# The first 13 units of the attention maxima, moved from the attention program to the end of the projection program

## What is computed

```python
h = _layernorm(x) * (1 + ca) + sa
q = concat([q_c, rope(q_e)]); k = concat([k_c, rope(k_e)])   # b, 16 heads, 2048, 16
scores = einsum('bhqd,bhkd->bhqk', q, k) * scale
scores = where(causal, scores, -inf)
att = softmax(scores)                                        # needs the row maxima
y = einsum('bhqk,bhkd->bhqd', att, v) @ Wc
```

## Time and profile before

| | us |
|---|---|
| median of 3 runs | 2794.07 (2793.2 to 2794.93) |
| profiled execution, its own time | 2799.72 |
| its span in the trace | 2798.0 |
| mean granted PE clock in it | 0.933 of full |

### The profile page before, as it was taken

The page is one execution under the profiler, slowest core; times in us unless marked ns, Lnnn a source line. Parts: engine busy times, 40 slices in busy tenths (PEclk is TensorE's granted clock), DMA queues, the critical chain, the costliest instruction groups (busy, mean ns, idle before and its releaser), DMA issues. The chain is left out here.

```text
span 2798.0 us, 46776 instructions
## 1 busy us (share of the span) xinstructions
PE 2536.4 (91%) x16092; PEld 1312.3 (47%) x16093; DVE 1906.6 (68%) x3194; ACT 1671.1 (60%) x2989; POOL 745.2 (27%) x692
## 2 busy tenths in 40 slices
PE   6985899999999999999999999999676579879898
PEld 4553233333333333333333333332265479779788
DVE  5985888878878878878888888781066556445433
ACT  2655037777777777777777777778532245435444
POOL 2544300111011011011011011011046747636533
PEclk8998579999999999999999999999887689989999
DMA  5798901541550451452353244000286666546434
GB/s 168 215 250 221 148 16 36 103 73 56 104 100 20 90 101 29 81 101 38 72 101 48 62 77 62 17 17 14 79 237 188 177 149 127 96 82 114 82 63 63
DMA packets 214886, 271.22 MB, mean 97 GB/s; under 512 B 27280, under 2 KB 176304, under 8 KB 212272
## 3 DMA queue, kind: packets, MB, share of 16 engines
q1 hardware_dynamic: 175408, 221.01, 35.8%
q0 software_dynamic: 32160, 41.57, 8.7%
q10 hardware_dynamic: 7136, 6.32, 0.7%
HBM read 136.30 MB, written 131.74 MB: 96 GB/s over the span
## 5 line engine op out<-in xcount | busy, mean ns | idle before, releaser
L1073 DVE TENSOR_REDUCE mxc<-ps 128x2 f32<-128x1024 f32 (+4 forms) x1168 | 1297.8, 1148 | 294.9 <-PE ps L981 182.6
L1054 ACT ACTIVATE probs<-ps 128x512 f32<-128x512 f32 (+1 forms) x2240 | 1184.3, 588 | 401.7 <-PE ps L1011 371.9
L1011 PE MATMUL ps<-qs,ks 99*128 99x512 bf16 (+3 forms) x2560 | 736.5, 350 | 6.5 <-ACT probs L1054 4.5
L981 PE MATMUL ps<-ks,qs 96*128 96x512 bf16 (+3 forms) x2560 | 696.7, 362 | 48.4 <-PEq L262 35.3
L1027 PE MATMUL ps<-probs,vs 128*32 128x512 f32 (+3 forms) x5120 | 600.0, 541 | 1.2 <-issue 0.5
L1011 PEld LDWEIGHTS ps<-qs,ks 99*128 99x128 bf16 x2560 | 216.1, 97 | 606.7 <-ACT probs L1054 461.2
L939 POOL TENSOR_SCALAR_AFFINE_SELECT probs<-probs 128x512 f32<-128x512 f32 x256 | 162.2, 634 | 993.3 <-ACT probs L1054 993.3
L981 PEld LDWEIGHTS ps<-ks,qs 96*128 96x128 bf16 x2560 | 240.7, 99 | 262.2 <-DVE mxc L1073 61.8
L1665 PE MATMUL ps<-x_t,w_at 128*128 128x128 f32 x2000 | 253.1, 281 | 9.3 <-ACT x_t L1696 8.4
L1665 PEld LDWEIGHTS ps<-x_t,w_at 128*128 128x128 f32 x2000 | 248.6, 197 | 22.1 <-issue 14.0
L1766 POOL DMA_INDIRECT out<-ys,idx x122 | 194.1, 1591 | 227.9 <-DMA out<-ys,idx 109.4
(11 more groups left out here) (172 smaller groups left out, 1830.2 us busy)
## 6 DMA issues: line engine op xcount, KB each, us to landing
ks<-k_parts SPq DMA_DIRECT2D x96, 256.0 KB, 13.0
qs<-q_parts SPq DMA_DIRECT2D x96, 256.0 KB, 14.6
xs<-slot_x SPq DMA_DIRECT2D x128, 131.0 KB, 2.1
v_ones<-vout SPq DMA_DIRECT2D x64, 256.0 KB, 3.5
vs<-v_ones SPq DMA_DIRECT2D x16, 1024.0 KB, 26.2
attn_t<-o_sb SPq DMA_DIRECT2D x64, 256.0 KB, 3.1
slot_x<-zero SPq DMA_DIRECT2D x24, 655.0 KB, 9.6
q_parts<-parts SPq DMA_DIRECT2D x96, 128.0 KB, 2.5
```

The source lines that it names most:

```text
L981: ins = pe.matmul(o[:, h, :], qs[r][0:SROWS, h0 + h, i * P:(i + 1) * P], ks[r][0:SROWS, h0 + h, 512 * c:512 * c + w], start=first, stop=no ...
L1011: ins = pe.matmul(o[:, h, :], ks[r][0:SROWS + MROWS, h0 + h, j * P:(j + 1) * P], qs[r][0:SROWS + MROWS, h0 + h, J * QJ + lo:(J + 1) * QJ], ...
L1054: act.activation(probs[:, (NKT * r + m) % NPB, h0:h0 + nh, 0:QJ - lo], st_view(r, s), ACT.Exp, scale=DH ** -0.5).then_inc(exp_done, 1)
L1073: dve.tensor_reduce(mxc[:, h0:h0 + nh, i, c], red_view(u, at), AX_X, ALU.max).then_inc(red_done, 1)
```

## The change

The list of units and the code of one unit become functions outside both programs (`unit_view`, `unit_products`, `unit_maxima`), with the same instructions. `mxc` and the two semaphores of the maxima are made before `project` and shared. In `project`, PE and DVE run units 0 to 12 (`HEAD`) of the first group after their last stage; in `attention` they skip these. The fill of `mxc` and the cast of the mask stand ahead of DVE's first full stage. `Course` and its order are as before.

```diff
+            g0["mxc"] = c2.enter_context(nc.sbuf_tensor("mxc", [P, HG, TT, 4], F32))
+            for n in ("ld", "red_ready", "red_done"):
+                g0[n] = ctx.enter_context(nc.semaphore(n + "0"))
+                retired.append(g0[n])
             project(nc, a, d, k, ps, g0, retired)
             attention(nc, a, d, k, ps, g0, retired)
...
+NRED = 2
+HEAD = len([u for u in UNITS if u[0] < 6])
+G_LD = 16 * 2 * len(COMBOS)
...
+def unit_products(pe, k, ps, ks, qs, u, at):
+
+    i, c, h0, nh, w = UNITS[u]
+    o, diag = unit_view(ps, u, at), c == i // 4
+    for h in range(nh):
+        first = w > 256 or h % (512 // w) == 0
+        ins = pe.matmul(o[:, h, :], qs[0:SROWS, h0 + h, i * P:(i + 1) * P], ks[0:SROWS, h0 + h, 512 * c:512 * c + w],
+                        start=first, stop=not diag, skip_group_check=w <= 256)
...
+def unit_maxima(dve, mxc, ps, u, at):
+
+    i, c, h0, nh, _ = UNITS[u]
+    return dve.tensor_reduce(mxc[:, h0:h0 + nh, i, c], unit_view(ps, u, at), AX_X, ALU.max)
...
                 dve.tensor_copy(k["identb"][:, :], k["ident"][:, :])
+                dve.memset(g0["mxc"][:, :, :, :], -3e38).then_inc(head_set, 1)
+                dve.wait_ge(ld_small, 16 * 2)
+                dve.tensor_copy(k["mask_qk"][:, :], mask_in[:, :]).then_inc(head_set, 1)
                 staged(dve, (0, normed), (2, rotate), (3, split))
-                dve.wait_ge(ld_small, 16 * 2)
-                dve.tensor_copy(k["mask_qk"][:, :], mask_in[:, :])
+                dve.wait_ge(head_set, 2)
+                for u in range(HEAD):
+                    dve.wait_ge(g0["red_ready"], u + 1)
+                    unit_maxima(dve, g0["mxc"], ps, u, u).then_inc(g0["red_done"], 1)
...
                 staged(pe, (1, transposes), (2, products))
+                pe.wait_ge(g0["ld"], G_LD)
+                pe.wait_ge(head_set, 2)
+                pe.wait_ge(copy_done, 2 * NB + 2)
+                pe.wait_ge(vcopy_done, NB + 1)
+                for u in range(HEAD):
+                    if u >= NRED:
+                        pe.wait_ge(g0["red_done"], u - NRED + 1)
+                    unit_products(pe, k, ps, g0["ks"], g0["qs"], u, u).then_inc(g0["red_ready"], 1)
...
-                    else:
+                    elif n > 0 or x >= HEAD:
                         group(n, x, unit_at[n, x])
...
-                dve.memset(mxc[:, :, :, :], -3e38).then_inc(init_done, 1)
-                dve.wait_ge(init_done, 1)
...
-                    else:
+                    elif n > 0 or u >= HEAD:
                         group(u, at)
```

More of the change, by code:

```diff
@@ L167, in build @@
             g0 = {n: c2.enter_context(nc.sbuf_tensor(n + "0", [P, HG, T], BF16)) for n in ("ks", "qs")}
-            g0["ld"] = ctx.enter_context(nc.semaphore("ld0"))
-            retired.append(g0["ld"])
+            g0["mxc"] = c2.enter_context(nc.sbuf_tensor("mxc", [P, HG, TT, 4], F32))
+            for n in ("ld", "red_ready", "red_done"):
+                g0[n] = ctx.enter_context(nc.semaphore(n + "0"))
+                retired.append(g0[n])
             project(nc, a, d, k, ps, g0, retired)
@@ L192, in build, with unit_view @@
                     experts(nc, d, k, r, w, zb, ps, out, h)
+UNITS = []
+for _i in range(TT):
+    for _c in range(_i // 4 + 1):
+        _w = min(512, P * (_i + 1) - 512 * _c)
+        _nh = HG if _w <= 256 and _i > 0 else 2
+        UNITS += [(_i, _c, _g, _nh, _w) for _g in range(0, HG, _nh)]
+NRED = 2
+HEAD = len([u for u in UNITS if u[0] < 6])
+G_LD = 16 * 2 * len(COMBOS)
+def unit_view(ps, u, at):
+    _, _, _, nh, w = UNITS[u]
+    buf = ps[:, 4:8, :].rearrange("p (u n) w -> p u n w", u=NRED)[:, at % NRED, :, :]
+    if w > 256:
+        return buf[:, :, 0:w]
+    return buf.rearrange("p n w -> p (n w)")[:, 0:nh * w].rearrange("p (h w) -> p h w", h=nh)
+def unit_products(pe, k, ps, ks, qs, u, at):
[5 more added lines that the diff above has]
+                        start=first, stop=not diag, skip_group_check=w <= 256)
+    if diag:
+        for h in range(nh):
+            ins = pe.matmul(o[:, h, w - P:w], k["identb"][:, :], k["mask_qk"][:, :],
+                            start=False, stop=True, skip_group_check=w <= 256)
+    return ins
+def unit_maxima(dve, mxc, ps, u, at):
+    i, c, h0, nh, _ = UNITS[u]
+    return dve.tensor_reduce(mxc[:, h0:h0 + nh, i, c], unit_view(ps, u, at), AX_X, ALU.max)
 def load_rows(sp, d, n, m, ks, qs, ld):
@@ L252, in project @@
         ld_down = [sem(f"s_down{x}") for x in range(3)]
+        head_set = sem("head")
         downs = ["L0_attn_Wq_down", "L0_attn_Wk_down", "L0_attn_Wv_down"]
@@ L768, in attention @@
         of_tile = [[s for s, x in enumerate(SETS) if x[0] == m] for m in range(NKT)]
[L770 to L775, removed]
+        GROUPS = UNITS
         NGRP = len(GROUPS)
@@ L779, in attention @@
         OUT_LAG = 2
-        NRED = 2
         assert NSET * R % NST == 0 and NKT * R % NPB == 0
@@ L795, in attention @@
         o_sb = sb("o_sb", [P, 2, QJ])
-        mxc, negm, res = sb("mxc", [P, HG, TT, 4]), sb("negm", [P, HG * TT]), sb("res", [P, 2, HG * TT])
+        mxc = g0["mxc"]
+        negm, res = sb("negm", [P, HG * TT]), sb("res", [P, 2, HG * TT])
         mparts = sb("mparts", [P, MROWS, HG * TT], BF16)
@@ L802, in attention @@
         v_ld = [sem(f"v{r}") for r in range(R)]
-        m_ld, pool_init, init_done, red_ready, red_done, neg_done, part_step, mt_done = (
-            sem(n) for n in ("mld", "pinit", "init", "redr", "redd", "neg", "part", "mt"))
+        red_ready, red_done = g0["red_ready"], g0["red_done"]
+        m_ld, pool_init, neg_done, part_step, mt_done = (sem(n) for n in ("mld", "pinit", "neg", "part", "mt"))
         st_ready, exp_done, mask_done, pv_done, o_done, zero_set, zero_st = (
@@ L815, in attention @@
         red_ps = ps[:, 4:8, :].rearrange("p (u n) w -> p u n w", u=NRED)
[L817 to L823, removed]
         def st_view(n, s):
@@ L971, in group @@
                 def group(n, u, at):
-                    i, c, h0, nh, w = GROUPS[u]
-                    r, o, diag = n % R, red_view(u, at), c == i // 4
+                    r = n % R
                     if u == 0:
@@ L978, in group @@
                         pe.wait_ge(red_done, at - NRED + 1)
[L979 to L988, removed]
+                    unit_products(pe, k, ps, ks[r], qs[r], u, at).then_inc(red_ready, 1)
                 def turn(n, at):
@@ L1065, in _ @@
             def _(dve):
-                dve.memset(mxc[:, :, :, :], -3e38).then_inc(init_done, 1)
-                dve.wait_ge(init_done, 1)
                 def group(u, at):
-                    i, c, h0, nh, w = GROUPS[u]
                     dve.wait_ge(red_ready, at + 1)
-                    dve.tensor_reduce(mxc[:, h0:h0 + nh, i, c], red_view(u, at), AX_X, ALU.max).then_inc(red_done, 1)
+                    unit_maxima(dve, mxc, ps, u, at).then_inc(red_done, 1)
                 def maxima(n, at):
```

## The result

| | before | after |
|---|---|---|
| median us | 2794.02 (4 runs, 2793.2 to 2794.93) | 2777.09 (4 runs, 2774.6 to 2782.1) |
| ratio | | 0.9942, 95% interval 0.9924 to 0.9959 |
| profiled execution, its time | 2799.72 | 2782.10 |
| its span | 2798.0 | 2780.4 |

The kernel is 16.9 us faster by these medians, 17.6 by the two profiled executions; 14.5 was forecast. The changed kernel's own runs spread over more than 7 us, so the size needed more runs. Over all runs of this study the changed kernel has 15 with a mean of 2779.3 us (standard error 0.9), the kernel before 45 with a mean of 2794.4 (0.4): 15.1 us less, give or take 1.9. Set against the runs of the kernel before that were taken beside them, the three measurements of the changed kernel differ by 16.3, 15.2 and 14.3 us in their means.

The account below looks back on a forecast made before the run. The first group's maxima, paced by DVE, were taken as a serial bound on the path. 14.90 us gained less 0.4 for the moved fill and cast gave 14.5, so 2794.07 - 14.5 = 2779.6 us, range 2775.0 to 2784.5.

Parts of the forecast that it names:

- Bound and path: First group's maxima, 285.1 to 372.5 us: DVE sets the pace, serial; a microsecond taken there is one of the kernel.
- Step 1: Attention's start: without units 0 to 12, unit 13's reduction starts at 286.17 instead of 301.07, gain 14.90 us.
- Step 2: Projection's tail: the moved units take 15.3 us, hidden by the stores' issuing and landing, 3.6 us to spare, cost nothing.
- Step 3: Projection's start: moved fill and cast delay PE, cost 0.4 us (0.10 to 0.48), passed on to the last stores.
- Step 4: Projection's tail: extra semaphore waits on PE and DVE lie before 266 or in the 3.6 us, cost nothing.
- the unshifted loads: Loads for groups 1 and 2 stay, ending just after 348; group 1 wants them near 358, over 9 us margin.
- The clock did not rise earlier: Rival, first group's maxima: PE working from 266 raises the clock earlier; half of 9.2 us gives 2775.0; chance 0.07.
- The tail fitted: Against the rival that DVE's moved units end 9.7 us past the stores, time 2789.3, half way 2784.5; chance 0.08.
- No stall of code: Against the rival that PE's or DVE's code arrives late at attention's start, 2804.0 up to 2823.5 us; chance 0.03.
- The range: Median of the whole kernel from 2775.0 to 2784.5 us, to hold 8 in 10 with the rivals.

Follow-up runs that it names:

- head16: The changed kernel with 16 units in the projection's tail instead of 13; 2776.74 us, ratio 0.9934.
- head20: The changed kernel with 20 units in the projection's tail instead of 13; 2775.39 us, ratio 0.9939.
- fill_pad: The changed kernel with one more DVE fill, of a spare 128 x 4096 tile, just ahead of the moved fill of `mxc`; 2782.17 us, ratio 0.9957.
- head40: The changed kernel with 40 units in the projection's tail instead of 13; 2794.75 us, ratio 0.9997.
- b_again: The kernel before, unedited, run once more for a second profile; a single execution of 2801.89 us, only its trace used.
- late_fill: The changed kernel with the fill and the cast put back behind DVE's last stage, ahead of the 13 units; 2782.37 us, ratio 0.9950.

## Why the prediction was right

- **Bound and path.** Right. The first group's maxima were a serial piece in which DVE sets the pace, and 15.0 us taken out of it came out of the kernel: 15.1 by the means over all runs.
- **Step 1, 14.90 us.** Measured 15.0 (87.43 and 87.42 against 72.38 to 72.44), of which the dropped fill is 0.10; the prediction had put that at nothing. Unit 13's reduction stands 1.05 behind attention's start (1.07).
- **Step 2, the cover.** Right: head of 15.3 us, 3.5 to spare (3.6). head16 and head20 show where it ends. The absolute times (`negm` near 358.0, first scores near 369.0) came some 2 us earlier, at 355.93 and 366.85, because that projection happened to be short.
- **Step 3, the moved fill and cast.** Sign and place right, size too small. The prediction took 0.4 and set an upper bound of 0.48 by adding two durations from where these instructions stood; it measured 0.8 to 1.0. fill_pad shows that a larger delay, of 3.8 us, passes to the end. With 0.9 in place of 0.4 the sum is 15.0 - 0.9 = 14.1; the runs, at 15.1 give or take 1.9, can't tell that from 14.5.
- **Step 4 and the unshifted loads.** Right for this change. head40 shows the loads' bound once they shift too, at the maxima's transfer, which the prediction did not list.
- **Rivals.** The clock did not rise earlier (0.50 to near 374, with PE busy 62.16 of 71.30 us in the maxima). The Trainium skill (TensorE: Matmul & The Clock Gate, on the clock gate) has sustained activity release the low clock; by this trace the moved units and the maxima together were not activity of that kind. The tail fitted. No stall of code: PE's first product stands 0.34 us ahead of SP's first transfer, as before (283.55 and 283.89, 285.10 and 285.44), and with 16, 19 and 20 units PE has only 1.3 to 2.4 us of idle time at the border and SP's first transfer stands as close behind it (0.33 to 0.34). The wait for code that the Trainium skill (Runtime: NRT & Kernel Launch, instruction fetch mechanics) lets one expect behind a jump shows at this border in none of the profiles.
- **The range.** The median of 2777.09 lies inside, 2.5 below the forecast. The scatter of the last piece and of the projection covers that. That the mean of all 15 runs, 2779.3, comes within 0.3 of the forecast is in part luck, since that mean is itself uncertain by 1.7 us either way. The run-to-run spread of 0.9 us that the range took from three runs was too small, since the 45 runs of the kernel before reach from 2789.65 to 2801.49.

## What to carry to other kernels

At a border between two programs look at who arrives last and what he waits for: here only SP, for stores to land, while two engines idled 19 and 35 us. Work whose inputs are long there can be moved into that time, up to the point where the slower of the engines arrives with SP (16 units here); past it a unit gained nothing (20 units), and once the next program's loads were pushed back far enough it lost (40 units). When one piece of a trace is exact and the others scatter by several us, compare the pieces first and the medians after.

## What the runs showed that was not expected

- Two tiny DVE instructions (0.27 and 0.21 us where they stood) cost 0.8 to 1.0 us in their new place; the cast lasted 0.48 there, and 0.21 before, beside other work of the start. The traces show where the time stands: the layernorm starts 0.13 us behind the start of `identb`'s cast before and 0.81 behind it after (38.10 and 38.91), which is 0.68; most of the rest is in the four scalings that make the normed tile (L349 before, L393 after), 2.13 us before, 2.31 in b_again and late_fill, 2.45 after. Why these instructions take longer there was not tried.
- The part behind attention takes from 888.4 to 898.1 us in kernels whose code there is the same, while the 1531 us of attention's main piece repeat within 1.5 in all profiles but head40's, which has the late transfer's standstill in it.
